# Row sums as one more operand column, scores turned once per half, and two mask tiles made early in a graph attention kernel

## The chip, the cores and the metric

The kernel runs on one core of one Trainium2 chip. The metric is the device time of one execution in microseconds (us). The kernel before takes 755.12 us (median of three runs, 754.40 to 755.93). Engines are called as in the profile: PE (matrix products), PEld (its weight loads), DVE (vector), ACT (scalar), POOL (GpSimd), SP (its queue issues most transfers).

## The reference

Cut to what matters (N = 2048 nodes, D = 512, 16 heads of 32):

```python
seq = (x @ W_seq).reshape(N, H, DH)
score1, score2 = einsum('nhd,d->hn', seq, a1), einsum('nhd,d->hn', seq, a2)
scores = leaky_relu(score1[:, :, None] + score2[:, None, :], 0.2)
attn = softmax(scores + (1 - adj) * -65500.0)
x1 = layernorm(x + elu(einsum('hij,jhd->ihd', attn, seq) @ W_out + b_out))
A = (adj + adj.T) * 0.5 + eye(N); deg = A.sum(1)
norm_adj = deg**-0.5 * A * deg**-0.5
out = layernorm(x1 + (adj @ norm_adj) @ x1)
```

The row sums of adj are needed for deg, and to see whether a node has no neighbour at all.

## The kernel before

The nodes are cut into 16 tiles of 128. A score is positive or not after the leaky relu, so exp(score) is one of two products of an exponential of the row and one of the column. Each head is therefore a product of the 0/1 adjacency (MT8, fp8) and of a masked step (G8: where the score is positive, and the edge exists) with small operand tables (PN, fp16, six groups of columns of DV = 33 numbers each: 32 features and one for the softmax sum).

**Stage one, the sequence products.** 32 products n (16 tiles for the lower eight heads, 16 for the upper) of eight matmuls each, `seq_product`, line 525. ACT copies each out of its bank (`move_seq`, line 731), POOL multiplies it with a1 and a2 (line 432), DVE reduces (`scores`, lines 860 and 862). After each product but the first three PE also turns one tile of score1 (`score_row`, line 536); ACT copies four of them at a time (`move_s1`, line 737), SP stores them to memory and reads each head's row back into all partitions (S1B; lines 329, 326). Meanwhile SP loads adj, 1 MB a tile, into four places (line 322), and ACT casts tile t to fp8 at the products listed in CAST_AT (line 726); a load waits until the cast four tiles before it is done. At fixed products DVE, PE and ACT work out the largest scores, the exponentials and the tables of the first half (`tops_of_rows`, `tops`, `exponents`, `tables`), and the operands of head 0 (`prep`, `high_operands`, `low_operands`: lines 913, 754, 920, 922).

**Stage two, the row sums.** PE multiplies each of the 256 blocks of adj with a column of ones (line 561).

**Stage three, 16 heads.** For each head h and tile j one step mask is made: on ACT (`Sign`, line 784, ten tiles of a head) or on DVE (line 961, the six tiles of OWN, made one tile ahead). DVE ands it with the adjacency (lines 974 and 978) into one of 16 places, and PE does 36 matmuls with it (lines 598 to 604). Between the tiles DVE puts its other work in an order written out by hand: the operands of the next head after tiles 4 and 11, the sums of the last head after tiles 8, 9, 10 and 13 (lines 927 to 952). In head 0 there are also `degrees` and `lone_nodes` (lines 1022 to 1032) after tiles 3 and 5, `tops_of_rows` and `tops` of the upper half, and `exponents`; PE turns the last scores after tile 3 and the tops after tile 6 (`second_half`), and ACT's last `move_s1` stands behind its mask for tile 8 and the operands of head 1. `choose_path` follows head 1 on DVE. PE may use a bank set again once the sums two heads before are out.

**Stage four** is the output product, the two normalisations and the two products with the adjacency. The change does not touch it.

Of the kernel before, what the change touches and what calls it, by code (L numbers as in the profile page):

```python
# [6 lines left out]
def gat_then_normalised_adjacency(nc, x, adj, w_seq, a1, a2, w_out, b_out, x_t, adj_t, adj_p, adj_tp, out, s1_rows, seq_copy):  # L7
# [19 lines left out]
    P = 128  # L27
# [24 lines left out]
    NV = NT - len(OWN)  # L52
    IB = 4
    NB = NT // IB
    CW = 3 * DV
    WW = 4 * DV
# [3 lines left out]
    ROW_BANK = (2, 3, 2, 3, 2, 3, 6, 7)  # L60
# [3 lines left out]
    LONE_AT = 128  # L64
    ACTZ = [j for j in range(NT) if j not in OWN]
# [4 lines left out]
    assert WW * (IB - 1) + CW <= 512 and 2 * NB == 8  # L70

    ctx = ExitStack()
    with ctx:
# [34 lines left out]
        PNB = 2 * NT * 6 * DV  # L108
        RP = sb("RP", [P, 3 * NT * P], f32)
        assert PNB // 2 + NT * 5 * DV <= 3 * NT * P  # L110
        PN = RP[:, 0:PNB // 2].bitcast(f16).rearrange("p (u t c d) -> p u t c d", u=2, t=NT, c=6)
        o = PNB // 2
# [7 lines left out]
        VMT = RP[:, 5280:5280 + NT * H].rearrange("p (t h) -> p t h", t=NT)  # L120
# [15 lines left out]
        s1T = W5[0:HH, :, :].rearrange("p k d -> p (k d)")  # L136
# [43 lines left out]
        row_ps = sem("row_ps")  # L180
# [113 lines left out]
        def wide_sums(u):  # L294

            return PS[:, u * NB:(u + 1) * NB, 0:(IB - 1) * WW].rearrange("p b (i e c) -> p b i e c", i=IB - 1, e=2)[:, :, :, 0, :]

        def narrow_sums(u):

            return PS[:, u * NB:(u + 1) * NB, (IB - 1) * WW:(IB - 1) * WW + 2 * DV]  # L300

        def wide_lows(u):

            return PS[:, u * NB:(u + 1) * NB, 0:(IB - 1) * WW].rearrange("p b (i e c) -> p b i e c", i=IB - 1, e=2)[:, :, :, 1, :]

        def narrow_lows(u):

            return PS[:, u * NB:(u + 1) * NB, (IB - 1) * WW + 2 * DV:(IB - 1) * WW + 3 * DV]

# [5 lines left out]
        def _(sp):  # L315
# [12 lines left out]
            def store_s1(e):  # L328
                sp.wait_ge(s1T_sb, (e + 1) * KC)
                sp.dma_start(s1_rows[e * HH:(e + 1) * HH, :], s1T).then_inc(s1_stored, 16)  # L330
# [32 lines left out]
            for h in range(2, H):  # L363
                sp.wait_ge(z_ready, (h - 1) * NV)
# [8 lines left out]
            sp.wait_ge(z_ready, (H - 1) * NV)  # L373
# [132 lines left out]
        def _(pe):  # L506
# [22 lines left out]
            def score_row(n):  # L529
                t, e, g = n % NT, n // NT, n // GT  # L530
                pe.wait_ge(s_sb, n + 1)
                if g >= 2 and t % GT == 0:
                    pe.wait_ge(s1T_sb, g - 1)
                if g == 6:
                    pe.wait_ge(vc_done, 1)
                last = tr(pb[ROW_BANK[g]][0:HH, (t % GT) * P:(t % GT + 1) * P], S1[:, e * HH:(e + 1) * HH, t], idf[:, :])
                if t % GT == GT - 1:
                    last.then_inc(s1T_ps, 1)
# [9 lines left out]
            for n in range(2 * NT):  # L548
                seq_product(n)
                if n >= 3:  # L550
                    score_row(n - 3)
# [12 lines left out]

            def second_half(j):
                if j == 3:
                    for n in range(2 * NT - 3, 2 * NT):
                        score_row(n)
# [4 lines left out]
                if j == 10:  # L573
                    pe.wait_ge(lone_done, 1)
                    mm(pb[5][:, LONE_AT:LONE_AT + 1], ones[:, :], LONES[:, :], start=True, stop=True)
                    spread_tops(1, pb[5])

            for h in range(H):
                u = h % 2
                pe.wait_ge(pn_ready, h + 1)  # L580
                if h == 0:
                    pe.wait_ge(s1T_sb, KC + 2)
                if h == 1:
                    pe.wait_ge(s1T_sb, 2 * KC)
# [3 lines left out]
                for j in range(NT):  # L588
                    s = (h * NT + j) % NG
                    pe.wait_ge(g_ready, h * NT + (j + 1))  # L590
                    high, low, edge = (PN[:, u, j, c:c + 2, :].rearrange("p c d -> p (c d)") for c in (0, 2, 4))
                    both = PN[:, u, j, 0:4, :].rearrange("p c d -> p (c d)")
                    for i in range(NT):
                        bank, c = pb[u * NB + i // IB], (i % IB) * WW
                        step, mask = G8[:, s, i * P:(i + 1) * P], MT8[:, j, i * P:(i + 1) * P]
                        ends = dict(stop=(j == NT - 1), skip_group_check=True)
                        if i % IB < IB - 1:
                            mm(bank[:, c:c + WW], step, both, start=(j == 0 and i % IB == 0), **ends)  # L598
                            last = mm(bank[:, c:c + WW].rearrange("p (e c d) -> p e c d", e=2, c=2)[:, :, 1, :], mask,  # L599
                                      PN[:, u, j, 4:6, :], start=False, **ends)  # L600
                        else:
                            mm(bank[:, c:c + 2 * DV], step, high, start=False, **ends)  # L602
                            mm(bank[:, c:c + 2 * DV], step, low, start=False, **ends)  # L603
                            last = mm(bank[:, c + DV:c + 3 * DV], mask, edge, start=False, **ends)  # L604
                    last.then_inc(g_used, 1)
                    if h == 0:
                        second_half(j)

# [111 lines left out]
        def _(sc):  # L720
# [12 lines left out]
            def move_s1(g):  # L733
                sc.wait_ge(s1T_ps, g + 1)
                if g == KC:
                    sc.wait_ge(s1_stored, 16)
                A(s1T[:, (g % KC) * 512:(g % KC + 1) * 512], pb[ROW_BANK[g]][0:HH, :], ACT.Copy).then_inc(s1T_sb, 1)
# [9 lines left out]
            def high_operands(h):  # L747
# [6 lines left out]
                A(PN[:, h % 2, :, 0:5:4, :], V2[:, :, :, :], ACT.Copy).then_inc(hi_ready, 1)  # L754

            for n in range(2 * NT):
                move_seq(n)
                if n % GT == 3 and n > GT:
                    move_s1((n - 7) // GT)
# [4 lines left out]
                if n in CAST_AT:  # L764
                    cast_adj(CAST_AT.index(n))

            def low_sums(h):

                sc.wait_ge(g_used, NG + (h + 1) * NT)
                if h >= 1:  # L770
                    sc.wait_ge(hid_done, h)
                A(TB[:, :, 0:IB - 1, :], wide_lows(h % 2), ACT.Copy).then_inc(low_sb, 1)
                A(TB[:, :, IB - 1, DV:2 * DV], narrow_lows(h % 2), ACT.Copy).then_inc(low_sb, 1)

            def att_head(h):

                u = h % 2
                sc.wait_ge(s1b_in[u], (h // 2 + 1) * 16 * NS)
                for j in range(NT):
                    if j in ACTZ:  # L780
                        m = h * NV + ACTZ.index(j)
                        if m >= NZ:
                            sc.wait_ge(g_ready, (m - NZ) // NV * NT + ACTZ[(m - NZ) % NV] + 1)
# [420 lines left out]
```

## Time and profile before

| | |
|---|---|
| time, median of 3 | 755.12 us |
| the profiled execution, its own time | 754.55 us |
| its span | 752.7 us |
| PE, PEld, DVE, ACT, POOL busy | 97%, 75%, 70%, 56%, 19% |
| masks on ACT, line 784 | 160 of 1993 ns |
| masks on DVE, line 961 | 96 of 1266 ns |
| ands on DVE, lines 974 and 978 | 256 of 676 and 681 ns |
| mean granted clock of PE | 0.989 |

Busy shares are of the whole span. PE's matmuls are pipelined and their ends are modelled, so its share says little; the start of a matmul is a real stamp. A row of DVE or ACT lasts a little longer than the engine is taken: the next one starts some 0.08 to 0.1 us before the row ends.

### The profile page before, as it was taken

To read this page: it belongs to the slowest core of one execution; us is meant where nothing else is said; L and a number is where in the kernel's file an instruction comes from. 1 tells how busy PE (TensorE), PEld (TensorE's weight loads), DVE (VectorE), ACT (ScalarE), POOL (GpSimd) and SP (SyncE) were. 2 spreads that over 40 slices of the span, in tenths; PEclk is the share of its full clock that TensorE was granted. 3 is DMA by queue.
4 is the path that set the end of the run, shared out by engine and by line. 5 is a ranking of instruction groups with operands and counts; after the bars stand their busy time and mean duration, and the time that the engine had idled before them with its cause. 6 is when DMAs were issued, how large, how long until landed. Compare 5 with 4: busy or idle time off the path is not lost.

```text
span 752.7 us, 24055 instructions
## 1 busy us (share of the span) xinstructions
PE 733.6 (97%) x10983; PEld 566.4 (75%) x10983; DVE 529.9 (70%) x866; ACT 424.2 (56%) x353; POOL 145.6 (19%) x166
## 2 busy tenths in 40 slices
PE   7998999999999999999999999999999999999996
PEld 5877999999999999999999996444344444444442
DVE  2578799999999999999999993788731101333332
ACT  2689879898898988989888962323221101000000
POOL 3556000001121312114000001575322100000000
PEclk9998799999999999999999999999999999999999
DMA  7995412413332443324211123895069500011001
GB/s 283 410 366 216 137 31 75 130 59 78 57 71 59 87 79 63 70 57 81 59 45 45 45 59 71 162 188 112 28 92 170 74 1 1 28 43 43 35 36 42
DMA packets 33302, 71.32 MB, mean 95 GB/s; under 512 B 3360, under 2 KB 13600, under 8 KB 31136
## 3 DMA queue, kind: packets, MB, share of 16 engines
q1 hardware_dynamic: 25136, 52.99, 20.2%
q0 software_dynamic: 8064, 16.78, 16.4%
q8 instruction: 86, 1.41, 0.7%
q14 instruction: 16, 0.13, 0.1%
HBM read 77.89 MB, written 8.65 MB: 115 GB/s over the span
## 4 chain that ended last, share of the span: by engine, by line
PE 84%; DVE 6%; DMA 3%; issue 3%; SPq 2%; ACT 1%; POOL 1%; POOLq 0%; DVEq 0%; ACTq 0%
PE bank L598 21%; PE bank L703 14%; PE bank L599 12%; PE bank L690 11%; PE bank L651 7%; PE bank L604 4%; PE bank L603 4%; PE bank L602 4%; DMA RG<-in_adj_t_dram 3%; PE bank L659 3%; DVE RZ L961 1%; PE bank L525 1%; ACT MT L726 1%; SPq L322 1%; PE bank L561 1%
## 5 line engine op out<-in xcount | busy, mean ns | idle before, releaser
L598 PE MATMUL bank<-RP,RG 128*128 128x132 f16 x3072 | 377.0, 221 | 0.2 <-DVE RG L974 0.2
L599 PE MATMUL bank<-RP,MT 128*128 128x66 f16 x3072 | 376.5, 197 | 0.0
L784 ACT ACTIVATE RZ<-RZ,TAB 128x2048 int8<-128x2048 f32 x160 | 306.5, 1993 | 18.4 <-DVE RG L974 17.6
L598 PEld LDWEIGHTS bank<-RP,RG 128*128 128x128 fp8e4 x3072 | 285.9, 98 | 0.6 <-DVE RG L974 0.3
L599 PEld LDWEIGHTS bank<-RP,MT 128*128 128x128 fp8e4 x3072 | 285.5, 98 | 0.0
L603 PE MATMUL bank<-RP,RG 128*128 128x66 f16 x1024 | 199.4, 195 | 0.0
L604 PE MATMUL bank<-RP,MT 128*128 128x66 f16 x1024 | 199.2, 195 | 0.0
L602 PE MATMUL bank<-RP,RG 128*128 128x66 f16 x1024 | 198.4, 194 | 0.0
L961 DVE TENSOR_SCALAR RZ<-RZ,TAB 128x2048 int8<-128x2048 f32 x96 | 121.5, 1266 | 0.0
L974 DVE TENSOR_TENSOR RG<-RZ,MT 128x512 int32<-128x512 int32 x160 | 108.2, 676 | 3.9 <-ACT RZ L784 3.9
L703 PE MATMUL bank<-RZ,MT 128*128 128x512 f16 x512 | 110.7, 379 | 0.0
L602 PEld LDWEIGHTS bank<-RP,RG 128*128 128x128 fp8e4 x1024 | 101.3, 99 | 0.0
L604 PEld LDWEIGHTS bank<-RP,MT 128*128 128x128 fp8e4 x1024 | 101.3, 99 | 0.0
L603 PEld LDWEIGHTS bank<-RP,RG 128*128 128x128 fp8e4 x1024 | 100.3, 98 | 0.0
L703 PEld LDWEIGHTS bank<-RZ,MT 128*128 128x128 fp8e4 x512 | 50.1, 98 | 60.4
L978 DVE TENSOR_TENSOR RG<-RZ,MT 128x512 int32<-128x512 int32 x96 | 65.4, 681 | 0.0
L1151 DVE SCALAR_TENSOR_TENSOR RZ<-bank,DSZ,RZ 128x512 f16<-128x512 f32 x16 | 11.7, 749 | 75.5 <-ACT RZ L845 75.5
L651 PE MATMUL bank<-RZ 128*128 128x512 f32 x128 | 57.9, 594 | 0.6 <-ACT RZ L802 0.6
L478 POOL TENSOR_TENSOR rstd<-vps,mhalf 128x1 f32<-128x1 f32 x32 | 24.6, 770 | 170.3 <-DVE vps L1117 170.3
L1162 DVE SCALAR_TENSOR_TENSOR W<-bank,SEQ 128x512 f32<-128x512 f32 x16 | 11.1, 691 | 63.6 <-PE bank L703 63.6
L690 PE MATMUL bank<-RG,RP 128*128 128x512 f16 x256 | 55.6, 379 | 0.0
L845 ACT ACTIVATE RZ<-bank,DSZ 128x512 f16<-128x512 f32 x16 | 10.7, 687 | 76.6 <-PE bank L690 74.1
(115 smaller groups left out, 793.8 us busy)
## 6 DMA issues: line engine op xcount, KB each, us to landing
RG<-in_adj_t_dram SPq DMA_DIRECT2D x16, 1024.0 KB, 8.5
RZ<-s_rows_dram SPq DMA_DIRECT2D x64, 256.0 KB, 3.3
seq_copy_dram<-SEQ SPq DMA_DIRECT2D x8, 528.0 KB, 4.6
RZ<-in_x_dram SPq DMA_DIRECT2D x16, 256.0 KB, 3.3
RP<-in_adj_p_dram POOLq DMA_DIRECT2D x8, 512.0 KB, 8.2
RP<-in_adj_tp_dram POOLq DMA_DIRECT2D x8, 512.0 KB, 12.3
out_dram<-W SPq DMA_DIRECT2D x16, 256.0 KB, 2.0
RQ<-in_x_t_dram SPq DMA_DIRECT2D x2, 1024.0 KB, 15.0
```

The source lines that it names most:

```text
L598: mm(bank[:, c:c + WW], step, both, start=(j == 0 and i % IB == 0), **ends)
L599: last = mm(bank[:, c:c + WW].rearrange("p (e c d) -> p e c d", e=2, c=2)[:, :, 1, :], mask, PN[:, u, j, 4:6, :], start=False, **ends)
L602: mm(bank[:, c:c + 2 * DV], step, high, start=False, **ends)
L603: mm(bank[:, c:c + 2 * DV], step, low, start=False, **ends)
L604: last = mm(bank[:, c + DV:c + 3 * DV], mask, edge, start=False, **ends)
L651: last = mm(pb[2 + t % 2][:, :], hT[:, t % 2, k * P:(k + 1) * P], WO[:, k, :], start=(k == 0), stop=(k == KC - 1))
L690: last = mm(pb[(t + NQ) % 8][:, :], panel(t)[:, j, :], XH[:, l, j, :], start=(j == 0 and l == 0), stop=(j == NT - 1 and l == 1))
L703: last = mm(pb[(t + NQ) % 8][:, :], MT8[:, j, t * P:(t + 1) * P], ZH[:, l, j, :], start=(j == 0 and l == 0), stop=(j == NT - 1 and l == 1))
L784: A(Z[:, m % NZ, :], S1B[u], ACT.Sign, bias=S2[:, h, j:j + 1], scale=-1.0).then_inc(z_ready, 1)
L961: V.tensor_scalar(ZD[:, (h * len(OWN) + m) % 2, :], S1B[u], S2[:, h, OWN[m]:OWN[m] + 1], -1.0, ALU.is_gt, ALU.mult).then_inc(zd_ready, 1)
L974: V.tensor_tensor(G32[:, s, :], Z32[:, m % NZ, :], MT32[:, j, :], ALU.bitwise_and).then_inc(g_ready, 1)
L978: V.tensor_tensor(G32[:, s, :], ZD32[:, m % 2, :], MT32[:, j, :], ALU.bitwise_and).then_inc(g_ready, 1)
```

## The change

It makes three changes at once. (1) The 256 row-sum matmuls go. In head 2 (ROW_HEAD) every operand group has a 34th column: 1 in one group, 0 elsewhere, so that the row sum of adj comes out of that head's products. DVE fetches it in `whole_sums(2)`, which in that head copies and adds in smaller pieces; `lone_nodes` moves to the end of head 3, `choose_path` behind it. (2) `score_row` goes: the scores of half the heads lie in one 128 x 128 square, turned by one transpose a half (after product 18, and after tile 5 of head 0) and copied by one ACT instruction. (3) Two masks of head 0 are made by ACT at products 27 and 30, tile 0's by DVE itself at product 28, with its and; tile 1's and comes at product 30. Tile 0 of head 0 joins DVE's own tiles. Some fixed places shift by one.

```diff
-    PE_TR, PE_TOP = 19, 21
-    EXP_AT, HIGH_AT = 22, 25
+    PE_S1, PE_TR, PE_TOP = 18, 18, 20
+    EXP_AT, HIGH_AT = 23, 26
+    EARLY_G = {28: 0, 30: 1}
+    EARLY_Z = {27: 2, 30: 3}
+    ROW_HEAD, LONE_HEAD = 2, 5
+    OWNS = ((0, 1, 4, 6, 9, 12, 14),) + (OWN,) * (H - 1)
...
-            def score_row(n):
...
+            def score_rows(e, bank):
+                pe.wait_ge(s_sb, (e + 1) * NT)
+                tr(bank[:, 0:P], S1[:, e * HH:(e + 1) * HH, :].rearrange("p h t -> p (h t)"), idf[:, :]).then_inc(s1T_ps, 1)
...
-            pe.wait_ge(seq_sb, 2 * NT - 1)
-            for j in range(NT):
-                pe.wait_ge(adjb_done, j + 1)
-                for i in range(NT):
-                    last = mm(pb[4][:, i:i + 1], MT8[:, j, i * P:(i + 1) * P], ones[:, 0:1], start=(j == 0 and i == 0),
-                              stop=(j == NT - 1), skip_group_check=True)
-            last.then_inc(row_ps, 1)
+            pe.wait_ge(seq_sb, 2 * NT - 2)
...
-                if j == 6:
+                if j == 5:
                     pe.wait_ge(seq_sb, 2 * NT)
-                    pe.wait_ge(row_sb, 1)
+                    score_rows(1, pb[6])
                     turn_tops(1, pb[4])
...
+                if n in EARLY_Z:
+                    step(0, EARLY_Z[n])
...
+                    if h == 0 and j == 7:
+                        move_s1(1, pb[6])
...
+                if h == ROW_HEAD:
+                    own.mark(V.memset(pn[:, :, :, DV], 0.0))
+                    own.wait(ve)
+                    own.mark(V.memset(pn[:, :, 4, DV], 1.0))
...
+                if h == ROW_HEAD:
+                    ve.wait_ge(low_row_sb, 2)
+                    d = DV + 1
+                    degrees(h)
+                    for c in range(2):
+                        cs = slice(c * DV, (c + 1) * DV)
+                        own.mark(V.tensor_tensor(TB[:, :, 0:IB - 1, cs], TB[:, :, 0:IB - 1, cs], wide(h, 0)[:, :, :, c * d:c * d + DV], ALU.add))
+                        own.mark(V.tensor_tensor(TB[:, :, IB - 1, cs], TB[:, :, IB - 1, cs], narrow(h, c, c + 1)[:, :, 0:DV], ALU.add))
+                    own.wait(ve)
+                    ve.sem_inc(banks_free, 2)
...
+                if h == ROW_HEAD + 1 and j == NT - 1:
+                    lone_nodes()
...
+                if n in EARLY_G:
+                    att_tile(0, EARLY_G[n])
```

## Rows read from the trace of the kernel before

**Rows 1.** Windows by stage: stretch, length, busy (instructions) by engine, granted clock, DMA

```profile
core 0: us, PE busy (x) PEld busy (x) DVE busy (x) ACT busy (x) POOL busy (x), PEclk, DMA share, GB/s
71.46:79.49 8.03, 6.82 (x259) 6.75 (x257) 7.28 (x14) 7.94 (x6) 1.39 (x2) 0.65 0.60 202
79.49:84.05 4.56, 4.56 (x68) 4.56 (x65) 4.50 (x11) 4.56 (x4) 0.00 (x0) 0.50 0.36 122
...
129.60:153.45 23.85, 23.70 (x576) 23.52 (x577) 23.69 (x35) 21.61 (x15) 0.00 (x0) 1.00 0.42 131
270.58:294.01 23.43, 23.43 (x581) 23.43 (x579) 23.27 (x34) 21.24 (x14) 3.85 (x4) 1.00 0.37 71
455.00:752.00 297.00, 287.37 (x1295) 133.50 (x1291) 118.20 (x231) 41.18 (x68) 61.71 (x83) 1.00 0.35 70
```

**Rows 2.** Timeline, tile 13 of heads 2 and 4: DVE's and, PE's first matmul

```profile
148.32 0.68 DVE L974 TENSOR_TENSOR RG<-RZ,MT 128x512 int32<-128x512 int32 x1
...
149.06 0.23 PE L598 MATMUL bank<-RP,RG 128*128 128x132 f16 x1 [0.15 <-DVE RG L974]
...
194.77 0.68 DVE L974 TENSOR_TENSOR RG<-RZ,MT 128x512 int32<-128x512 int32 x1
...
195.92 0.22 PE L598 MATMUL bank<-RP,RG 128*128 128x132 f16 x1
```

**Rows 3.** Waits in 71 to 106 us: engine, line, released by: us, times, longest

```profile
DVE RG L974 <- ACT RZ L784: 3.9, 3, 2.7
ACT W L737 <- PE bank L536: 3.2, 1, 3.2
...
DVE TOPS L879 <- PE bank L542: 1.2, 1, 1.2
...
DVE TAB L862 <- POOL RP L432: 0.7, 2, 0.5
```

**Rows 4.** Timeline of ACT in stage one: cast, high operands, copy

```profile
58.85 1.89 ACT L726 ACTIVATE MT<-RG 128x2048 fp8e4<-128x2048 f32 x1
...
61.36 1.13 ACT L754 ACTIVATE RP<-RP 128x1056 f16<-128x1056 f32 x1 [0.26 <-DVE RP L913]
62.39 0.36 ACT L731 ACTIVATE SEQ<-bank 128x256 f32<-128x256 f32 x1
```

**Rows 5.** Timeline of SP's queue: the loads of score rows, then adj tiles 12 to 15

```profile
48.70 1.75 SPq L326 DMA_DIRECT2D RZ<-s_rows_dram  x4
50.49 8.54 SPq L322 DMA_DIRECT2D RG<-in_adj_t_dram  x4
```

**Rows 6.** The adj loads of line 322, all 16

```profile
DMA to landing us min/median/max: 6.7/8.5/18.9
```

**Rows 7.** Timeline, POOL's last products and DVE beside them; the same DVE line later

```profile
39.82 1.19 POOL L432 TENSOR_TENSOR RP<-SEQ,AV 128x512 f32<-128x512 f32 x1 [0.57 <-ACT SEQ L731]
...
67.60 2.82 POOL L432 TENSOR_TENSOR RP<-SEQ,AV 128x512 f32<-128x512 f32 x2 [1.44 <-ACT SEQ L731]
...
68.08 1.30 DVE L922 TENSOR_SCALAR RP<-RP 128x1056 f16<-128x1056 f16 x1
...
69.63 0.67 DVE L862 TENSOR_REDUCE TAB<-RP 128x16 f32<-128x512 f32 x1
...
95.95 0.43 DVE L922 TENSOR_SCALAR RP<-RP 128x1056 f16<-128x1056 f16 x1
```

**Rows 8.** Groups of DVE from 70 to 105.8 us: busy us, mean ns, idle before

```profile
L961 DVE TENSOR_SCALAR RZ<-RZ,TAB 128x2048 int8<-128x2048 f32 x8 | 10.2, 1278 | 0.0
L974 DVE TENSOR_TENSOR RG<-RZ,MT 128x512 int32<-128x512 int32 x12 | 8.2, 686 | 3.9 <-ACT RZ L784 3.9
...
L913 DVE TENSOR_TENSOR RP<-SEQ,TAB 128x528 f32<-128x528 f32 x2 | 1.3, 700 | 0.0
L860 DVE TENSOR_REDUCE RP<-SEQ 128x8 f32<-128x256 f32 x3 | 1.2, 404 | 0.0
...
L1022 DVE COPY ROW<-bank 128x16 f32<-128x16 f32 x1 | 0.2, 169 | 0.0
```

**Rows 9.** Timeline of DVE in head 2: the sums of head 1

```profile
139.01 0.97 DVE L927 TENSOR_TENSOR RP<-RP,bank 128x792 f32<-128x792 f32 x1
139.90 0.42 DVE L928 TENSOR_TENSOR RP<-RP,bank 128x264 f32<-128x264 f32 x1
```

More of the change, by code:

```diff
@@ L69, in gat_then_normalised_adjacency @@
     AT_LOWS = 9
-    assert WW * (IB - 1) + CW <= 512 and 2 * NB == 8
+    assert (4 * (IB - 1) + 3) * (DV + 1) <= 512 and 2 * NB == 8
     ctx = ExitStack()
@@ L597, in _ @@
                         if i % IB < IB - 1:
-                            mm(bank[:, c:c + WW], step, both, start=(j == 0 and i % IB == 0), **ends)
-                            last = mm(bank[:, c:c + WW].rearrange("p (e c d) -> p e c d", e=2, c=2)[:, :, 1, :], mask,
-                                      PN[:, u, j, 4:6, :], start=False, **ends)
-                        else:
-                            mm(bank[:, c:c + 2 * DV], step, high, start=False, **ends)
-                            mm(bank[:, c:c + 2 * DV], step, low, start=False, **ends)
-                            last = mm(bank[:, c + DV:c + 3 * DV], mask, edge, start=False, **ends)
+                            mm(bank[:, c:c + 4 * d], step, both, start=(j == 0 and i % IB == 0), **ends)
+                            last = mm(bank[:, c:c + 4 * d].rearrange("p (e c d) -> p e c d", e=2, c=2)[:, :, 1, :], mask,
+                                      pn[:, 4:6, :], start=False, **ends)
+                        else:
+                            mm(bank[:, c:c + 2 * d], step, high, start=False, **ends)
+                            mm(bank[:, c:c + 2 * d], step, low, start=False, **ends)
+                            last = mm(bank[:, c + d:c + 3 * d], mask, edge, start=False, **ends)
                     last.then_inc(g_used, 1)
@@ L765, in _ @@
                     cast_adj(CAST_AT.index(n))
[L767 to L778, printed above, removed]
-                for j in range(NT):
[L780 to L783, printed above, removed]
-                        A(Z[:, m % NZ, :], S1B[u], ACT.Sign, bias=S2[:, h, j:j + 1], scale=-1.0).then_inc(z_ready, 1)
+                if n in EARLY_Z:
+                    step(0, EARLY_Z[n])
+            for h in range(H):
+                for j in range(NT):
+                    if j in ACTS[h] and not (h == 0 and j in EARLY_Z.values()):
+                        step(h, j)
                     if j == AT_HIGH and h < H - 1:
@@ new lines, in att_tile @@
+            def att_tile(h, j):
+                if j == 0 and 0 in OWNS[h]:
+                    own_step(h, 0)
+                if j + 1 in OWNS[h]:
+                    own_step(h, j + 1)
+                masked(h, j)
+                if h == LONE_HEAD + 1 and j == AT_EVAC + 1:
+                    count_lone()
+                if h > 0 and j == AT_EVAC + 1:
+                    whole_sums(h - 1)
+                if h > 0 and j == AT_EVAC + 2:
+                    scale_sums(h - 1)
+                    add_sums(h - 1)
+                if h > 0 and j == AT_EVAC + 3:
+                    norms(h - 1)
+                if j == AT_PREP and h < H - 1:
+                    prep(h + 1)
+                if j == AT_LOW and h < H - 1:
+                    low_operands(h + 1)
+                if h > 0 and j == AT_HID:
+                    hidden_head(h - 1)
+                if h == 0 and j == 3:
+                    tops_of_rows(1)
+                if h == 0 and j == 9:
+                    tops(1, pb[4])
+                if h == 0 and j == 13:
+                    exponents(1, pb[5])
+                if h == 1 and j == 3:
+                    tables(1)
+                if h == ROW_HEAD + 1 and j == NT - 1:
+                    lone_nodes()
@@ L1005, in _ @@
+            def att_head(h):
+                for j in range(NT):
+                    if not (h == 0 and j in EARLY_G.values()):
+                        att_tile(h, j)
             for n in range(2 * NT):
@@ L1043, in choose_path @@
                 V.tensor_scalar(FLAG[:, :], WID[:, 2:3], 0.0, None, ALU.is_gt).then_inc(flag_ready, 1)
-            for h in range(2):
+            for h in range(H - 1):
                 att_head(h)
-            choose_path()
-            for h in range(2, H - 1):
-                att_head(h)
+                if h == LONE_HEAD + 1:
+                    choose_path()
             ve.wait_ge(pow_done, 1)
```

239 lines of the change are left out of this document (114 added, 125 removed).

## The prediction

> **What bounds the kernel now.** I read the windows by stage first [rows 1]. The last 297 us (stage four) are not edited, so the change can only move the moment at which the 16 heads end. In the heads both PE and DVE look full: in head 8, 23.43 us long, DVE is busy 23.27 us of it and PE all of it. PE does a tile in 23.43 / 16 = 1.46 us. Which of the two sets the end must be read from distances: how long after DVE's and has ended does PE start on that tile [rows 2]? In head 2, tile 13, the and ends at 148.32 + 0.68 = 149.00 and PE, idle for 0.15 us, starts at 149.06: PE waits for DVE. In head 4, tile 13, the distance is 195.92 - 195.45 = 0.47 us, and later it grows: DVE needs slightly less for a head than PE. So DVE sets the time up to head 2, PE from there on. A microsecond taken from PE before head 2 is worth nothing unless DVE comes earlier too.
>
> The Trainium skill (Perfetto Trace Analysis, Identifying the Most-Contended Engine) has PE judged by its weight loads and not by its matmuls; here the loads are busy 23.52 of 23.85 us in head 2 and 23.43 of 23.43 in head 8, which would make PE the bound in both. Of head 2 the distance of 0.06 us says otherwise; what that reading would give is the second rival below.
>
> **Removed.** The row sums hold PE for 8.03 us at a granted clock of 0.65, and head 0 then begins with 4.56 us at 0.50, 1.2 GHz [rows 1]. On DVE: one copy (0.08 us). On ACT and PE seven of eight score copies and 30 of 32 turnings, which lie beside the loads of adj. What matters to DVE is its idle time between 71 and 106 us: 3.9 us for ACT's masks (three times), 1.2 for the turned tops (once), 0.7 for POOL (twice) [rows 3]. Of these ACT's first comes from the copy that stood in its queue for 3.2 us until PE had turned the last scores [rows 3]. With the 0.08 us by which rows overlap (six idle stretches) the sum is 5.8 + 0.5 = 6.3 us. `lone_nodes` and `choose_path` cost the same in head 3 as before; both are paid ahead of head 4, tile 13, before and after.
>
> **When head 0 can begin.** I walk ACT's queue. The cast of adj tile 12 stands at product 24. Its load is issued at 50.49 behind four loads of score rows [rows 5] and lands 6.7 to 8.5 us later [rows 6]: 57.2 to 59.0; I take 58.1. Before, the cast ran at 58.85 [rows 4], so ACT has almost nothing to win here, however fast PE gets. From there: cast 1.89, two copies 0.52, operands 1.02, cast 1.89, copy 0.26, cast 1.89, the early mask of tile 2 1.89: product 28 is copied from 67.5 on. Then its copy 0.37, POOL's product 1.19 [rows 7] and DVE's reduce 0.60: DVE is through with score 28 at 69.75. Before that was 0.59 after 69.63, at 70.22 [rows 7]. **Gain 0.47 us**, from 0 if the load lands at 59.0 to 1.4 if at 57.2.
>
> Now DVE makes two masks, 2 x 1.19, and the and, 0.60 [rows 8] (less the overlap): PE gets tile 0 at 72.75. PE has been through with its products since about 66 us, so it stands idle for over 6 us and will begin at the lower clock. Three more scores (0.33 + 0.60 each), the ands of tiles 1, 2 and 3, the mask of tile 4 and `tops_of_rows` (1.05) end at 79.55; tile 4, `prep` (1.24), the mask of tile 6 and tile 5 end at 83.2. PE ends tile 5 at 84.8, the turned scores are copied at 85.4, and only behind that copy does ACT make the mask of tile 8: 87.4.
>
> **New stalls of DVE.** It is through with tile 7 and the mask of tile 9 at 85.6, and waits 1.7 us for tile 8. ACT next makes the operands of head 1 and tile 10's mask (1.02 + 1.98): 90.3, while DVE is ready at 89.1: 1.2 us. Then each mask of ACT comes 1.89 us after the last: 0.1 us at tile 11 and some 0.7 at tiles 2 and 3 of head 1, where it waited twice before. Together 3.7 us. **Gain 6.3 - 3.7 = 2.6 us.**
>
> **Added to DVE.** The mask of tile 0, 1.19. In head 1 two memsets with a wait between: no such pair is in the rows; below a copy of 0.08 each, above 0.5; I take 0.26. In `whole_sums(2)` four adds in place of two. Rows of 792 and 264 numbers take 0.89 and 0.34 us [rows 9], so 1.04 ns a number and 0.065 us at the start; four adds of 396, 132, 396, 132 take 1.36 in place of 1.23. With two copies (0.16), the wait for their end and the count (0.18) that is 0.47, from 0.2 to 1.0. Minus the copy of before, 0.08. **Loss 1.84 us.** The 34th column makes PE's 198 columns a block 204, 3% of 23.4 us, at most 0.7 us in head 2; DVE is the later one there, so it is hidden. If PE were the bound it would cost 0.7.
>
> **POOL beside the early masks.** POOL works on product 29 when DVE wants its first mask, and on 30 when it wants the second. In the rows `low_operands`' last step takes 1.30 us beside POOL, whose two products take 2.82 in place of 2 x 1.19, and 0.43 when POOL is idle [rows 7]: 0.9 us lost for one meeting. Below 0 (they miss each other), above two meetings, 0.4 for the product under way and 1.2 for the next, with some 0.3 at the ands after: 2.0. I take one meeting: **loss 0.9 us.**
>
> The Trainium skill (SBUF — State Buffer, Who interferes with whom) speaks against this part of the change: a vector instruction in a two-port mode and a GpSimd instruction take turns at a shared pair of ports, each for its whole length. The rows agree, in that the loss is about one POOL product. By that rule both masks would wait and the loss would be the upper end.
>
> **Sum.** DVE reaches head 4, tile 13 earlier by 0.47 + 2.6 - 1.84 - 0.9 = 0.33 us. There it had 0.47 us of distance, of which all but 0.06 can be used: PE, and with it the end, comes 0.33 + 0.41 = 0.74 us earlier. Against the profiled execution that is 754.55 - 0.7 = 753.8; the median of the runs is 0.6 above it, so **754.4**. Head 2, tile 13 is not the bound: neither the sums of head 2 (0.47) nor `lone_nodes` and `choose_path` have been paid there.
>
> SP: the store of the upper scores waits for ACT's copy at 85.4 and stands ahead of the score rows of head 2 only. POOL: its power waits for `lone_nodes`, now in head 3, far ahead of head 15.
>
> **Rivals.**
> - *It pays more on DVE.* No meeting with POOL (0.9 more), or tile 12 landing at 57.2 (0.9 more), or both: 753.5 to 752.6. For it: the meeting hangs on tenths of a microsecond. Chance 0.22.
> - *PE is the bound after all.* Then PE's earlier start counts in full: 79.49 - 73.65 = 5.8 us, 749.3, and with the clock up to 2.3 us more. Against it stands the distance of 0.06 us. Chance 0.06.
> - *Slower: PE is still at 1.2 GHz when tile 5 comes.* Its place is the copy that gates ACT's mask of tile 8. At half clock a tile takes 36 x 4.56 / 68 = 2.4 us in place of 1.46 [rows 1], so if that clock lasts past 84.5 us the whole chain is 1 us late, and if it has held since tile 0, with tiles 0 to 5 back to back, 73.65 + 6 x 2.4 = 88.1 against 85.7: 2.4 us, and PE has more to catch up. 755.8 to 757.5. For it: six idle microseconds and then gaps between tiles. Against it: head 0 got its clock back after 4.56 us of work before. Chance 0.13.
> - *Slower: the additions are dearer.* Both meetings (1.1 more) and the dearer sums and memsets (0.8 more): 755.2 to 756.3. Chance 0.17, of which half is slower by the bound.
> - *The forecast*, 753.7 to 755.3. Chance 0.42. It includes that the row sums go and nothing follows, since DVE lends in head 0 what it pays back in head 3.
>
> **The numbers.** About 0.2%, 1.5 us, is what a measurement of this kernel can tell from no change. Faster by more: the first two rivals, most of them (0.25), and the edge of the forecast (0.07): 0.32. Slower by more: 0.12 of the third and 0.09 of the fourth: 0.21. Within: 0.47. The range is 751.8 to 757.2: from the first rival with 0.8 for the unknown stalls, to the third; the second is left out. The likeliest case alone is 753.7 to 755.3.
>
> **What would show it.** PE's first head matmul starts at 72.7 to 74.5 at a granted clock of 0.5. DVE waits for ACT at tiles 8 and 10 of head 0, 1.5 and 1.2 us. A mask of line 961's kind takes over 1.3 us while POOL multiplies. The smallest distances are in head 4 and not in head 2, and near 0.06 us; from head 5 on they grow again and PE takes 23.42 us a head. The prediction is wrong if the distances stay above 0.3 us in all of heads 3 and 4, if ACT's queue does not wait for the copy of the scores, or if stage four changes its length.

## The result, and the profile after

The changed kernel takes 756.91 us (median of 14 runs, 753.96 to 758.83), the kernel before in the same session 755.15 (14 runs): ratio 1.0021, 95% interval 1.0012 to 1.0031. By the ratio it is slower by 1.6 us, where 0.7 us less was forecast. The row sums (8.03 us of PE) are gone, and the time went up. The profiled execution took 757.03 us, span 755.2, mean granted clock 0.992.

The windows by stage of the changed kernel, which answer to [rows 1]:

```profile
core 0: us, PE busy (x) PEld busy (x) DVE busy (x) ACT busy (x) POOL busy (x), PEclk, DMA share, GB/s
68.60:76.56 7.96, 0.00 (x0) 0.03 (x1) 6.61 (x8) 7.96 (x9) 4.31 (x3) 0.62 0.40 132
76.56:80.70 4.14, 4.14 (x56) 4.10 (x57) 4.14 (x9) 2.04 (x2) 1.17 (x1) 0.50 0.37 131
82.00:84.00 2.00, 2.00 (x55) 2.00 (x52) 1.93 (x6) 0.00 (x0) 0.00 (x0) 1.00 0.26 92
...
249.22:273.17 23.95, 23.76 (x581) 23.52 (x578) 23.79 (x35) 21.52 (x14) 7.32 (x6) 1.00 0.39 69
273.17:296.60 23.43, 23.43 (x582) 23.43 (x579) 23.27 (x34) 21.23 (x14) 3.24 (x5) 1.00 0.38 71
```

The first line answers to the first of [rows 1]: where PE had done row sums it now stands idle for 8 us and waits for DVE. Head 0 begins at 76.56 in place of 79.49, at 1.2 GHz. Head 8 begins at 273.17 in place of 270.58, 2.59 us late; from there on both kernels do a head in 23.43 us, and the span ends 2.5 later. So everything happened ahead of head 8. Where does DVE set the time there? The same places as in [rows 2], tile 13 of head 4 and then of head 7:

```profile
197.20 0.68 DVE L1003 TENSOR_TENSOR RG<-RZ,MT 128x512 int32<-128x512 int32 x1
...
197.94 0.23 PE L584 MATMUL bank<-RP,RG 128*128 128x132 f16 x1 [0.15 <-DVE RG L1003]
...
268.04 0.68 DVE L1003 TENSOR_TENSOR RG<-RZ,MT 128x512 int32<-128x512 int32 x1
...
268.78 0.23 PE L584 MATMUL bank<-RP,RG 128*128 128x132 f16 x1 [0.15 <-DVE RG L1003]
```

In head 4 the distance fell from 0.47 to 0.06 us (197.94 - 197.20 - 0.68), as forecast, but DVE is 2.43 us later there (197.20 against 194.77) and not 0.33 earlier. Head 7 has a second tight place, which was not forecast: 23.95 us for that head against 23.43.

Where DVE lost its time is seen ahead of head 0. ACT's timeline, which answers to [rows 4]:

```profile
56.69 0.36 ACT L721 ACTIVATE SEQ<-bank 128x256 f32<-128x256 f32 x1
60.46 1.91 ACT L716 ACTIVATE MT<-RG 128x2048 fp8e4<-128x2048 f32 x1 [3.41 <-DMA RG<-in_adj_t_dram]
...
67.95 2.00 ACT L766 ACTIVATE RZ<-RZ,TAB 128x2048 int8<-128x2048 f32 x1
69.84 0.65 ACT L721 ACTIVATE SEQ<-bank 128x256 f32<-128x256 f32 x2
...
89.09 0.28 ACT L725 ACTIVATE W<-bank 128x128 f32<-128x128 f32 x1 [10.49 <-PE bank L535]
89.27 1.99 ACT L766 ACTIVATE RZ<-RZ,TAB 128x2048 int8<-128x2048 f32 x1
```

The cast of tile 12 is the second line. Before, it began at 58.85 right behind ACT's earlier work; now ACT stands idle for 3.41 us until the load lands. SP's timeline of the same stretch, which answers to [rows 5], shows why it lands late:

```profile
45.47 0.33 SPq L334 DMA_DIRECT2D s_rows_dram<-W  x1
45.84 0.43 SPq L326 DMA_DIRECT2D RG<-in_adj_t_dram  x1
50.30 1.75 SPq L330 DMA_DIRECT2D RZ<-s_rows_dram  x4
52.09 5.05 SPq L326 DMA_DIRECT2D RG<-in_adj_t_dram  x4
```

SP's queue waits at the score rows until their store has landed: from 45.47 to 50.30, and tile 12 stands behind them. Behind that wait the DMA engines run low (windows of 50 to 52 us, the changed kernel and then the one before). In the next 2 us the kernel before has its own dip, a share of 0.70 beside 0.91; over 44 to 60 us it moved about a tenth more bytes.

```profile
50.00:52.00 2.00, 2.00 (x11) 1.77 (x10) 1.93 (x7) 0.66 (x3) 1.23 (x1) 1.00 0.38 143
```

```profile
50.00:52.00 2.00, 2.00 (x12) 1.67 (x11) 1.34 (x3) 0.38 (x1) 1.19 (x2) 1.00 0.90 268
```

DVE's timeline from the last reduce ahead of the early masks, with its stalls in head 0:

```profile
71.52 0.69 DVE L859 TENSOR_REDUCE TAB<-RP 128x16 f32<-128x512 f32 x1 [0.84 <-POOL RP L436]
72.12 3.70 DVE L993 TENSOR_SCALAR RZ<-RZ,TAB 128x2048 int8<-128x2048 f32 x2
75.74 0.68 DVE L1007 TENSOR_TENSOR RG<-RZ,MT 128x512 int32<-128x512 int32 x1
...
78.18 1.03 DVE L1007 TENSOR_TENSOR RG<-RZ,MT 128x512 int32<-128x512 int32 x1
...
91.39 0.69 DVE L1003 TENSOR_TENSOR RG<-RZ,MT 128x512 int32<-128x512 int32 x1 [1.77 <-ACT RZ L766]
...
94.28 0.69 DVE L1003 TENSOR_TENSOR RG<-RZ,MT 128x512 int32<-128x512 int32 x1 [1.15 <-ACT RZ L766]
```

And POOL beside the masks:

```profile
70.30 4.43 POOL L436 TENSOR_TENSOR RP<-SEQ,AV 128x512 f32<-128x512 f32 x3 [2.87 <-ACT SEQ L721]
```

DVE is through with score 28 at 72.12 (before 70.22, forecast 69.75). The two masks last 3.70 us where 2.48 was their plain time (twice 1.28 less the overlap), and three products of POOL 4.43 where they need 3 x 1.18. One by one the masks take 1.58 and 2.19 us and the products 1.18, 1.18 and 2.00. The waits at tiles 8 and 10 are 1.77 and 1.15 us, for 1.7 and 1.2 forecast. PE had until 76.56 nothing to do but wait for tile 0.

One caution for all readings below: the stream of adj loads runs up to 2.4 us earlier or later from one profiled execution to the next (the cast of tile 8 begins at 44.95 in the kernel before and at 47.30 in one that differs only behind it), and all stamps behind it move along. I therefore measure from the cast of tile 8 (at 44.95 before, 45.32 after, which the change does not reach) to that of tile 12: 13.9 us before, 15.1 after. In the four kernels below that equal the changed one up to there the distance is 14.8, 14.9, 15.5 and 16.9 us. What lies behind the load of tile 12 I measure from the cast of tile 12.

### The profile page after: what moved, and what is told of

Read it like the earlier page. It is cut to its first block, busy times and chain, and to the rows that moved or that the text cites. A ratio compares the mean times of both kernels' runs of the same rounds, so it can differ in the third digit from the quotient of the medians.

```text
span 755.2 us, 23476 instructions
## 1 busy us (share of the span) xinstructions
PE 724.6 (96%) x10697; PEld 559.4 (74%) x10697; DVE 531.4 (70%) x872; ACT 418.7 (55%) x347; POOL 146.5 (19%) x166
## 4 chain that ended last, share of the span: by engine, by line
PE 75%; DVE 13%; issue 5%; DMA 2%; ACT 2%; POOL 1%; SPq 0%; ACTq 0%; POOLq 0%; DVEq 0%
PE bank L584 17%; PE bank L693 14%; PE bank L680 11%; PE bank L585 10%; PE bank L641 7%; DVE RZ L993 4%; PE bank L590 3%; PE bank L589 3%; PE bank L529 3%; PE bank L649 3%; PE bank L588 3%; DVE RG L1003 2%; DVE RG L1007 2%; DMA RG<-in_adj_t_dram 1%; POOL RP L436 1%
## 5 line engine op out<-in xcount | busy, mean ns | idle before, releaser
L584 PE MATMUL bank<-RP,RG 128*128 128x132 f16 (+1 forms) x3072 | 377.4, 221 | 12.6 <-DVE RG L1007 10.4
L585 PE MATMUL bank<-RP,MT 128*128 128x66 f16 (+1 forms) x3072 | 376.6, 196 | 0.0
L589 PE MATMUL bank<-RP,RG 128*128 128x66 f16 (+1 forms) x1024 | 199.5, 195 | 0.0
L590 PE MATMUL bank<-RP,MT 128*128 128x66 f16 (+1 forms) x1024 | 199.2, 195 | 0.0
L588 PE MATMUL bank<-RP,RG 128*128 128x66 f16 (+1 forms) x1024 | 198.3, 194 | 0.0
L993 DVE TENSOR_SCALAR RZ<-RZ,TAB 128x2048 int8<-128x2048 f32 x97 | 124.1, 1280 | 0.0
L693 PEld LDWEIGHTS bank<-RZ,MT 128*128 128x128 fp8e4 x512 | 50.1, 98 | 60.4
L842 ACT ACTIVATE RZ<-bank,DSZ 128x512 f16<-128x512 f32 x16 | 10.7, 687 | 76.6 <-PE bank L680 74.1
## 6 DMA issues: line engine op xcount, KB each, us to landing
RG<-in_adj_t_dram SPq DMA_DIRECT2D x16, 1024.0 KB, 10.7
```

What stands on the lines that cost most here:

```text
L584: mm(bank[:, c:c + 4 * d], step, both, start=(j == 0 and i % IB == 0), **ends)
L585: last = mm(bank[:, c:c + 4 * d].rearrange("p (e c d) -> p e c d", e=2, c=2)[:, :, 1, :], mask, pn[:, 4:6, :], start=False, **ends)
L588: mm(bank[:, c:c + 2 * d], step, high, start=False, **ends)
L589: mm(bank[:, c:c + 2 * d], step, low, start=False, **ends)
L590: last = mm(bank[:, c + d:c + 3 * d], mask, edge, start=False, **ends)
L693: last = mm(pb[(t + NQ) % 8][:, :], MT8[:, j, t * P:(t + 1) * P], ZH[:, l, j, :], start=(j == 0 and l == 0), stop=(j == NT - 1 and l == 1))
```

## The experiments

All were timed in five rounds beside the kernel before. "after" is the changed kernel; ratios are to the kernel before (median 754.85 us of 30 runs for the first four, 754.97 of 23 for the next four, 755.85 of 23 for the last four), where the changed kernel, measured beside its own runs of the kernel before, stands at 1.0021. A ratio has an interval of about 0.0010 to 0.0016 to either side.

**The debt of heads 3 to 7.** Row sums, lone nodes and path are moved from where DVE is short to where it has 1.5 us of distance.

```diff
-    ROW_HEAD, LONE_HEAD = 2, 5
+    ROW_HEAD, LONE_HEAD = 10, 13
```

> The changed kernel with the 34th column in head 10 in place of head 2 and the count of lone nodes after head 13 in place of 5, so that DVE's extra work falls where it is 1 us and more ahead of PE. Theory A (DVE's ledger: what DVE took over is paid back in heads 3 and 6, where PE then waits for it): the distances in heads 3 to 7 stay above 0.3 us, PE does not wait after head 1, and the heads end about 1.2 us earlier than in the changed kernel, 755.7 us. Theory B (the loss is PE's: the lower clock of head 0 and the wider columns): nothing of that moves, 756.9 us.

Measured: 755.47 us (12 runs), 1.0010 [0.9999, 1.0021]. Heads 2 to 7 take 23.43 us each and no distance there is near 0.06; the ratio is 0.0011 lower than the changed kernel's, 0.8 us. The two intervals overlap, so the times alone do not show it, but the profile has the same account: head 7 no longer costs its 0.52, head 4 not its 0.44, and head 1 takes 25.03 us for 25.47. Not all of it is hidden in the new place: heads 10, 13 and 14 take 23.52, 23.45 and 23.67 us, 0.35 more than three others. From the cast of tile 12 to the end of the heads it is 1.3 us less than in the changed kernel. It is a part of the loss, by the medians not the greater part.

**No early tiles.** The two masks of ACT, the two of DVE and tile 0's move to DVE are undone.

```diff
-    EARLY_G = {28: 0, 30: 1}
-    EARLY_Z = {27: 2, 30: 3}
-    OWNS = ((0, 1, 4, 6, 9, 12, 14),) + (OWN,) * (H - 1)
+    EARLY_G = {}
+    EARLY_Z = {}
+    OWNS = (OWN,) * H
```

> The changed kernel without its third part: no mask and no and before the last product, tile 0 of head 0 back on ACT. Theory A: DVE is rid of one mask (1.2 us) and of the meetings with POOL (1.6 us), and loses the time in which it waited for scores anyway (about 1 us): some 1.8 us earlier, 755.1 us, though PE begins head 0 at the same time or later. Theory B: PE begins later at the lower clock, so not faster than 756.9 us.

Measured: 755.66 us (12 runs), 1.0013 [1.0000, 1.0026]. Head 0 begins at 75.72, which looks earlier than the 76.56 of the changed kernel, but the load of tile 12 was earlier too: from the cast of tile 12 (59.50 here, 60.46 there) it is 16.2 us without the early tiles and 16.1 with them. So they do not let PE begin sooner. Behind that, head 0 takes 27.44 us in place of 29.38, since in the changed kernel three of DVE's scores still stand behind tile 0, and the heads end 1.8 us sooner after that cast, as the first theory had it; by the ratios the time is only 0.6 us less. Part 3 of the change is thus no gain in this kernel. That it is a loss the times do not show: the interval reaches to the changed kernel's ratio.

**Part 2 alone**, on the kernel before: one turn, one copy and one store a half.

```diff
-            def score_row(n):
...
+            def score_rows(e, bank):
+                pe.wait_ge(s_sb, (e + 1) * NT)
+                tr(bank[:, 0:P], S1[:, e * HH:(e + 1) * HH, :].rearrange("p h t -> p (h t)"), idf[:, :]).then_inc(s1T_ps, 1)
...
-                sp.dma_start(s1_rows[e * HH:(e + 1) * HH, :], s1T).then_inc(s1_stored, 16)
+                sp.dma_start(s1_rows.rearrange("h (t p) -> (h t) p", p=P)[e * P:(e + 1) * P, :], s1T[:, e, :]).then_inc(s1_stored, 16)
```

> The kernel before with the second part alone: the scores of each half turned by one transpose, one ACT copy and one store of 128 rows of 512 bytes; row sums by PE as before, no early tiles. Theory A (the store of 128 short rows waits behind the load of adj tile 10 in every queue, so the score rows and adj tile 12 come 1.5 us and more later): the cast of adj tile 12 waits for its load by more than 1 us and DVE is through with score 28 later than 70.2; 755.2 to 757 us, since the row sums hide part. Theory B (the late load is another part's doing or chance): the cast does not wait, 754 to 755 us.

Measured: 757.08 us (7 runs), 1.0034 [1.0020, 1.0048]: as slow as the whole change or slower. It takes 30 turnings and 6 copies away and loses 2.6 us. ACT's timeline of this kernel:

```profile
57.77 0.36 ACT L719 ACTIVATE SEQ<-bank 128x256 f32<-128x256 f32 x1
61.13 1.91 ACT L714 ACTIVATE MT<-RG 128x2048 fp8e4<-128x2048 f32 x1 [3.00 <-DMA RG<-in_adj_t_dram]
```

The same hole of 3 us ahead of tile 12 stands here without any early mask or missing row sum. The hole is not the loss, though: part 2 also brings ACT to this cast earlier, and from the cast of tile 8 (46.77) to that of tile 12 there are 14.4 us, 0.5 more than before. DVE's waits for ACT's masks between 71 and 106 us are 5.0 us in three, where they were 3.9 [rows 3]. Head 8 begins at 272.53, 1.95 us later than before, but 1.82 of these lie ahead of the cast of tile 8, within what the stream of loads varies by. Most of the 2.6 us of the medians is thus not located by this one profile.

**The order of the loads.** Only SP's queue is changed: the score rows go behind adj tile 15.

```diff
-                if t == 12:
-                    sp.wait_ge(s1_stored, 16)
-                    for q in range(NS):
-                        load_s1(0, q)
                 load_adj(t)
+            sp.wait_ge(s1_stored, 16)
+            for q in range(NS):
+                load_s1(0, q)
```

> The changed kernel with the loads of head 0's score rows behind all adj tiles in SP's queue, in place of ahead of tile 12. Theory A: adj tile 12 lands before 58 us and its cast does not wait; but the score rows land at about 67 us, and the early mask of tile 2 at product 27 waits for them with all later copies behind it on ACT: half of the 2.3 us comes back, 755.5 to 756.3 us. Theory B: 756.9 us.

Measured: 754.73 us (12 runs), 0.9998 [0.9986, 1.0010]: the loss is gone. ACT's timeline:

```profile
56.05 1.90 ACT L715 ACTIVATE MT<-RG 128x2048 fp8e4<-128x2048 f32 x1
...
65.01 2.00 ACT L765 ACTIVATE RZ<-RZ,TAB 128x2048 int8<-128x2048 f32 x1 [1.37 <-DMA RZ<-s_rows_dram]
```

From the cast of tile 8 (44.4) to that of tile 12 there are now 11.6 us, and no wait. The price is a wait of 1.37 for the score rows at ACT's first early mask. Head 0 begins at 73.62, and from the cast of tile 8 to the start of head 8 it is 2.0 us less than in the changed kernel (225.9 for 227.9). It stays an equal of the kernel before; heads 0 and 1 still wait for ACT, 3.5 us in three waits as in the changed kernel.

**POOL held back.** Product 30 on POOL also waits for the and of tile 0, so that it can't meet DVE's second mask.

```diff
                 if n >= 2:
                     gp.wait_ge(s_sb, n - 1)
+                if n == 30:
+                    gp.wait_ge(g_ready, 1)
```

> The changed kernel with one more wait: POOL's product 30 waits until the and of tile 0 is done, so that it can't run beside DVE's two early masks. Theory A (POOL and DVE take turns, a length each): the second early mask takes 1.3 us in place of 2.2, PE starts head 0 about 1 us earlier, and with it the whole chain, 755.9 us. Theory B (the long masks have another cause): the second mask still takes about 2.2 us and the time stays at 756.9 us or rises, since POOL is held up.

Measured: 756.30 us (12 runs), 1.0011 [0.9999, 1.0023]. DVE's and POOL's timelines:

```profile
70.17 2.77 DVE L995 TENSOR_SCALAR RZ<-RZ,TAB 128x2048 int8<-128x2048 f32 x2
...
68.35 2.31 POOL L438 TENSOR_TENSOR RP<-SEQ,AV 128x512 f32<-128x512 f32 x2 [2.87 <-ACT SEQ L723]
...
73.71 2.32 POOL L438 TENSOR_TENSOR RP<-SEQ,AV 128x512 f32<-128x512 f32 x2 [3.05 <-DVE RG L1009]
```

The two masks take 2.77 in place of 3.70 and POOL's products their plain 1.16 each: the contention is confirmed as a mechanism, at 0.93 us, and PE begins head 0 15.2 us after the cast of tile 12 where it was 16.1. Of the time the intervals say only that the gain lies between nothing and some 2 us.

**The second copy of the scores later.** ACT's last copy goes behind its mask for tile 10, so it no longer holds the mask of tile 8.

```diff
-                    if h == 0 and j == 7:
+                    if h == 0 and j == 10:
                         move_s1(1, pb[6])
```

> The changed kernel with ACT's copy of the upper scores behind its mask for tile 10 of head 0 in place of tile 5 and 7, so that the masks of tiles 8 and 10 don't wait for PE to end tile 5. Theory A (DVE sets the time in heads 0 and 1): the waits of 1.8 and 1.2 us at tiles 8 and 10 go, the heads end 2 to 3 us earlier, 754.4 us. Theory B (PE sets it): less than 0.5 us, 756.5 us.

Measured: 753.70 us (12 runs), 0.9982 [0.9972, 0.9992], 3 us less than the changed kernel and faster than the one before. DVE's waits from 71 to 106 us, the changed kernel and then this one (engine, line, released by: us, times, longest):

```profile
DVE RG L1003 <- ACT RZ L766: 2.9, 2, 1.8
DVE TAB L859 <- POOL RP L436: 0.8, 1, 0.8
```

```profile
DVE TAB L859 <- POOL RP L436: 0.8, 1, 0.8
DVE RG L1003 <- ACT RZ L766: 0.6, 1, 0.6
```

The 2.9 us are gone (the 0.6 left is that of head 1, which in the changed kernel comes behind 106 us), and 2.9 us is what the kernel gained by the ratios: DVE and ACT, not PE, set heads 0 and 1.

**Everything together**: rows last, debt late, copy later, and EARLY_Z = {} (no early mask of ACT). The second kernel also gives tile 1 back to its place and tile 0's mask back to ACT: only tile 0's and is early, at product 30.

```diff
-    EARLY_Z = {27: 2, 30: 3}
+    EARLY_Z = {}
```

> The changed kernel with the score rows loaded behind all adj tiles, the 34th column in head 10, the count after head 13, the copy of the upper scores behind the mask of tile 10, and the early masks of ACT (tiles 2 and 3) behind the last copy. Theory A: each repair counts, since each shortens DVE's chain: 2.9 for the load, 1.2 for the later debt, 2 to 3 for the copy, together some 6 us less than the changed kernel: 750 to 751.5 us. Theory B: PE's lower clock in head 0 holds most of it back, 753.5 us or more.

```diff
-    EARLY_G = {28: 0, 30: 1}
-    OWNS = ((0, 1, 4, 6, 9, 12, 14),) + (OWN,) * (H - 1)
+    EARLY_G = {30: 0}
+    OWNS = (OWN,) * H
```

> As e7, and tile 0 of head 0 is back on ACT, its and at product 30: DVE has no early mask of its own ahead of tile 0. Theory A: 1.2 us for the mask and the meetings with POOL go, about 1.5 us less than e7: 749 to 750 us. Theory B: no gain over e7.

Measured: 747.41 us (4 runs), 0.9895 [0.9880, 0.9911], and 746.34 (4 runs), 0.9881 [0.9866, 0.9897]. Both are better than was expected. Windows of the second, nearly its heads 0 and 1:

```profile
71.93:99.00 27.07, 27.07 (x588) 26.95 (x589) 26.22 (x46) 22.61 (x17) 0.00 (x0) 0.89 0.30 99
99.60:123.00 23.40, 23.40 (x580) 23.40 (x578) 23.17 (x35) 23.40 (x16) 0.00 (x0) 1.00 0.22 67
```

PE no longer waits for DVE in heads 0 and 1: head 0 begins at 71.93 and the heads end at 450.66, where the kernel before had 79.49 and 457.96. Of the 7.6 us by which PE starts earlier 7.3 arrive at the end. That is what an earlier start was worth once DVE's and ACT's chain was out of the way. How much of it is due to the removal of the row sums is not shown, since this kernel was not tried with them kept. The nearest is a kernel of the last session below, the one before with part 2 and the same order of loads: it keeps the row sums and begins head 0 at 74.35, 18.5 us after its cast of tile 12, where this one needs 15.5.

**Why so much more?** Four kernels of a last session. First the order of the loads, on the kernel before and on the one with part 2 alone:

```diff
-                if t == 12:
-                    sp.wait_ge(s1_stored, 16)
-                    for q in range(NS):
-                        load_s1(0, q)
                 load_adj(t)
+            sp.wait_ge(s1_stored, 16)
+            for q in range(NS):
+                load_s1(0, q)
```

> The kernel before, with nothing of the change; only the score rows are loaded behind adj tile 15. Theory A (the score rows are a cost by their place, with short or long stores alike): tile 12 lands at about 54 in place of 58.3, ACT's queue moves up, head 0 cannot start before the row sums are done (they hold PE), so DVE gains little: the ratio to before is 0.995 to 1.000. Theory B (only the 128 short rows of the changed store are harmful, the place does not matter to before): tile 12 lands earlier but DVE's free time and the end stay within 0.3 us, 0.9995 to 1.0005.

> Part 2 alone (one turn, one copy and one store a half) on the kernel before, with the score rows loaded behind adj tile 15. It lost 2.6 us with the rows ahead of tile 12 (1.0034). Theory A (the loss of part 2 is that the score rows and tile 12 stand behind the store): tile 12 lands at about 54, the loss goes, and the kernel stands within 0.2% of the kernel before with the same order. Theory B (the loss is ACT's one late copy of the scores behind the turn in head 0, which gates the masks of tiles 8 and 10): it stays 1.5 to 2.5 us slower than that kernel.

Measured: 755.28 us (12 runs), 0.9989 [0.9975, 1.0003], and 754.03 (12 runs), 0.9987 [0.9976, 0.9999]. For the kernel before the order is worth nothing that can be told; 0.9989 lies in the range of the first theory and the interval reaches into that of the second, so neither falls. Its ACT still needs 13.9 us from the cast of tile 8 to that of tile 12, since there the cast stands behind ACT's own work. With part 2 those are 11.6 us, and part 2, which lost 0.34% with the old order, loses nothing (0.9987 beside 0.9989). So by the times its loss goes with the place of the score rows; the late copy, which both part-2 kernels have, is not what sets it apart. The profiles do not say how: from the cast of tile 8 to the start of head 8 the two part-2 kernels need 225.8 us (old order) and 225.9, because in the second DVE waits 8.4 us for ACT's masks where it was 5.6, and the 2.6 us between their casts of tile 8 (46.77 and 44.18) lie ahead of the edit. For the changed kernel itself time and profile agree, 1.7 and 2.0 us.

Then the parts of the good kernel, on the changed one with the score rows behind tile 15. The first of the two has both of these edits, the second only the later copy:

```diff
-                    if h == 0 and j == 7:
+                    if h == 0 and j == 10:
...
-    EARLY_Z = {27: 2, 30: 3}
+    EARLY_Z = {}
```

> The combination that reached 0.9895 (747.4 us), but with the row sums taken in head 2 and the node counts in head 5 and 6, as in the changed kernel. Theory A (up to head 2 DVE has won 7 to 8 us, so PE and not DVE is late by the time head 5 comes; the counts then lie beside PE): 747.4 to 748.3, within 0.1% of the combination. Theory B (the debt is paid in any case ahead of head 7, as 1.1 us were with the changed kernel): 748.4 to 749.2.

> The changed kernel with two edits: the score rows loaded behind adj tile 15 and the second copy of the scores behind tile 10's mask. Alone they gave 2.3 and 3.2 us against the changed kernel. Theory A (they shorten one chain of DVE and ACT in heads 0 and 1, one after the other, and add up): 5 to 6 us less than the changed kernel, 751 to 752. Theory B (together they give more than the sum, since the debt of heads 3 to 7 then lies in DVE's distance): under 750.5. Theory C (they answer to the same stall): over 753.

Measured: 749.28 us (5 runs), 0.9914 [0.9900, 0.9929], and 751.67 (6 runs), 0.9949 [0.9933, 0.9964]. The steps from the changed kernel are

| kernel | ratio | step, us |
|---|---|---|
| changed | 1.0021 | |
| score rows last | 0.9998 | -1.7 |
| and the copy later | 0.9949 | -3.7 |
| and no early masks on ACT | 0.9914 | -2.6 |
| and the debt late | 0.9895 | -1.4 |
| and one early tile only | 0.9881 | -1.1 |

(a ratio step times 755, between kernels of different sessions). The intervals of the first three steps do not overlap, those of the last two do. ACT's early masks are the step that had not been counted. ACT's timeline of the two kernels at the same place, with the masks and then without:

```profile
65.76 2.00 ACT L765 ACTIVATE RZ<-RZ,TAB 128x2048 int8<-128x2048 f32 x1 [1.16 <-DMA RZ<-s_rows_dram]
67.67 0.64 ACT L720 ACTIVATE SEQ<-bank 128x256 f32<-128x256 f32 x2
68.20 1.91 ACT L715 ACTIVATE MT<-RG 128x2048 fp8e4<-128x2048 f32 x1
```

```profile
65.30 0.66 ACT L720 ACTIVATE SEQ<-bank 128x256 f32<-128x256 f32 x2
65.82 1.93 ACT L715 ACTIVATE MT<-RG 128x2048 fp8e4<-128x2048 f32 x1
```

The mask waits for the score rows and then holds the copies that POOL and DVE wait for: they come at 67.67 in place of 65.30, 10.7 us after the cast of tile 12 in place of 7.5. Head 0 begins at 74.37 with them and at 72.98 without; counted from the cast of tile 12 (57.01 and 57.83) that is 17.4 against 15.2, 2.2 us, and no more comes behind. The medians say 2.6, with intervals that allow about 0.3 to 4.8. The debt is 1.4 us here beside 0.8 with the changed kernel. Head 4 takes 23.87 us and head 7 23.93 in the kernel that keeps it, as in the changed one, so it is paid in full as expected by the second theory.

## Why the prediction was wrong

**Right.** DVE and not PE set the time in heads 0, 1 and 4, so the 8 us that PE was rid of came to nothing, and the second rival (749.3) did not occur. The stalls of tiles 8 and 10 (1.77 and 1.15 for 1.7 and 1.2) and one of 0.60 in head 1, 3.5 in sum for 3.7. Head 0 begins at 1.2 GHz, though at 76.56 and not at 72.7 to 74.5, and has 2.4 GHz back by 82 us; the distances behind DVE's ands are 0.06 to 0.70 us on tiles 1 to 5, and 0.06 on tile 5, whose end the copy of the scores waits for, so PE kept up and the third rival fell. The 34th column costs PE 0.09 us and not 0.7: head 2 takes 23.52 us, as head 10 does in the kernel that has the column there, where head 2 takes 23.43. The smallest distance of heads 3 and 4 is 0.06, that of head 2 is 0.32.

**The step that failed** is "Its load is issued at 50.49 behind four loads of score rows". That stamp was taken over from before, although part 2 changes the store which those four loads wait for. It was issued at 52.09 and took 8.3 us (to 60.4, at the upper end of the 6.7 to 8.5 that was used, where 7.6 stood in the sum). The term "gain 0.47" measured a loss of 1.90: 2.37 us off, the greater part of the 3.3 by which head 8 misses (2.59 late in place of 0.74 early). Some 0.4 us of it is the adj stream of this execution (the cast of tile 8), which is no effect of the change. With the order of the loads as the only edit 1.7 us came back, and part 2 alone, which lost 2.6 us, loses nothing with the same order, though there the profiles do not show where the time lies.

Why is the store slower? Before it writes 8 rows of 8 KB, now 128 of 512 bytes. From the store's issue to the first score-row load there were 3.6 us before, and in six kernels with the new store 3.9, 3.9, 4.8, 4.9, 4.9 and 4.9. The store is not all of it: the load of tile 12 behind it took 7.8 us before and 7.9 to 9.9 in these six. That the short rows do it was argued and not tried: a store of the same size in long rows would need the old turning.

**Mis-sized.** *POOL beside the early masks*, loss 0.9: DVE's three rows there are longer by 0.30 (first mask, 1.58), 0.92 (second) and 0.35 (the and at 78.18), 1.57 together, so two meetings and not one. By the Trainium skill (SBUF — State Buffer, Who interferes with whom) a DVE instruction in a two-port mode and a GpSimd instruction exclude each other for the whole of either. The trace agrees: both masks waited, and POOL's third product took 2.00 us for 1.18. The upper end of 2.0, which the prediction set for that case, was nearer than its 0.9. Holding POOL back gave 0.93 of it back in the trace. *Memsets* of head 1: from the and ahead of them (121.68) to the first row of `low_operands` behind them (122.84) there are 1.16 us, where without them it would be the 0.60 of an and, so 0.56 for 0.26; 0.28 of it is waiting. *Sums* of head 2, in DVE's timeline of head 3:

```profile
163.42 0.16 DVE L943 COPY ROW<-bank 128x12 f32<-128x12 f32 x1
...
164.72 0.28 DVE L933 TENSOR_TENSOR RP<-RP,bank 128x132 f32<-128x132 f32 x1
165.22 0.69 DVE L1007 TENSOR_TENSOR RG<-RZ,MT 128x512 int32<-128x512 int32 x1 [0.22 <-DVE RP L933]
```

1.80 us from the copy to the next and, where the same work takes 1.22 in head 4: 0.58 for 0.47.

**Misread.** "`lone_nodes` and `choose_path` cost the same in head 3 as before; both are paid ahead of head 4": `choose_path` follows head 6. Its five rows on DVE,

```profile
246.31 0.17 DVE L1064 TENSOR_TENSOR RV<-VC 128x16 f32<-128x16 f32 x1
...
247.10 0.15 DVE L1072 TENSOR_SCALAR FLAG<-WID 128x1 int32<-128x1 f32 x1
247.17 1.28 DVE L993 TENSOR_SCALAR RZ<-RZ,TAB 128x2048 int8<-128x2048 f32 x1
```

take 0.86 us (246.31 to 247.17) just ahead of head 7, whose distances had not grown by then. The section on the change, which has it behind `lone_nodes`, is wrong in the same way. Of the 2.59 us 2.02 are there at tile 13 of head 4 (197.94 against 195.92) and 0.52 come in head 7. Smaller slips: six of the eight score copies went and not seven; the terms that lead to 69.75 add up to 69.66; and by [rows 1] DVE is busy 23.69 us in head 2, more than the 23.52 of the weight loads, so the busy times name DVE there as the distance does, and only in head 8 PE.

The balance for DVE at tile 13 of head 4: forecast 0.33 early; 2.37 for the load, 0.67 for POOL, 0.30 and 0.11 for memsets and sums, minus 0.2 for the stalls and minus 0.86 for the path that is not yet paid, give 2.06 late. Measured are 2.43; 0.4 stays unassigned. Most of the miss is the one term: without its 2.37 DVE would be 0.06 late there and head 8 0.2, which is no gain and no loss that could be told. The time lies inside the range of 751.8 to 757.2 by luck, since the slow end of that range was set for a clock that did not come. No rival had the load: of the two slower ones the clock did not occur, and the dearer additions (755.2 to 756.3) had a part in it.

## What to carry to other kernels

When an instruction that a queue waits for is changed (here a store that four loads stand behind), work out anew every stamp behind that wait, on every queue; none may be taken from the trace of before. An engine that is not late gains nothing by an earlier start until the late chain is shortened, and then nearly all of it arrives (7.3 of 7.6 us): look for the edits that make the chain short before the removal is judged. A stamp of one execution is compared with that of another only from a common event close ahead of it: the start of head 0 without the early tiles was 0.8 us earlier as it stands and 0.1 later from the cast of tile 12. An instruction that is put ahead of others in a strict queue costs what stands behind it, and early work for an idle engine is worth nothing where it delays the input of the next.

## What the runs showed of the hardware

- A mask of 128 x 2048 on DVE beside POOL's product took 2.19 us in place of 1.27, and that product 2.00 in place of 1.18: both sides pay.
- Four loads of score rows and the store ahead of them left the DMA engines at a share of 0.38 for 2 us; the deepest dip of the kernel before in that stretch was 0.70, and the changed kernel with the score rows last had none (0.99 to 1.03 from 46 to 56 us).
- PE at 1.2 GHz for the first 4 us of head 0 set nothing, since DVE was no faster; where DVE was out of the way (the best kernel) the clock's mean over head 0 was 0.89 and PE was busy all the time, so the clock would be the next thing to look at there. That was not tried.
